# Routed expert tiles: rows read by transposing DMAs from SyncE in place of TensorE transposes

## What is computed

```python
probs = jax.nn.sigmoid(flat @ router_w.T)
scores, idx = jax.lax.top_k(probs, TOPK)
w = scores / (jnp.sum(scores, axis=-1, keepdims=True) + 1e-06)
h = jnp.maximum(jnp.einsum('td,edh->teh', flat, ew1) + eb1[None, :, :], 0.0)
eo = jnp.einsum('teh,eho->teo', h, ew2) + eb2[None, :, :]
routed = jnp.einsum('teo,te->to', eo, comb)
return shared + routed.reshape(b, s, -1)
```

## Time and profile before

| | us |
|---|---|
| median of 3 executions | 700.69 |
| lowest, highest | 696.97, 701.76 |
| profiled execution, its own time | 701.35 |
| its span in the profile | 699.1 |
| routed tiles, first hidden matmul of r0 to the end of r16 | 462.68 to 674.49 |

### The profile page before, as it was taken

The page is one execution under the profiler, slowest core; times in us unless marked ns, Lnnn a source line. Parts: engine busy times, 40 slices in busy tenths (PEclk is TensorE's granted clock), DMA queues, the critical chain, the costliest instruction groups (busy, mean ns, idle before and its releaser), DMA issues. The chain is left out here.

```text
span 699.1 us, 19138 instructions
## 1 busy us (share of the span) xinstructions
PE 601.9 (86%) x6150; PEld 500.8 (72%) x6150; DVE 484.6 (69%) x1304; ACT 394.0 (56%) x994; POOL 287.0 (41%) x327
## 2 busy tenths in 40 slices
PE   2689999999999999999757999989979989899950
PEld 2457777787777778777536888778868878688850
DVE  5858778877877877778695866565654746556537
ACT  4468888888888888887716423253533434324320
POOL 7303344443443334446530077405535534456120
PEclk9799999999999999999975999999999999899995
DMA  8525557775555655633050042213343332441218
GB/s 226 148 79 145 154 135 190 193 187 131 133 133 137 138 141 138 154 87 68 1 181 1 8 153 99 90 42 128 103 154 119 91 120 91 112 145 46 61 49 311
DMA packets 86600, 84.28 MB, mean 121 GB/s; under 512 B 17879, under 2 KB 80341, under 8 KB 86430
## 3 DMA queue, kind: packets, MB, share of 16 engines
q1 hardware_dynamic: 78686, 70.83, 37.5%
q0 software_dynamic: 2976, 8.16, 3.2%
q10 hardware_dynamic: 4896, 4.76, 2.7%
HBM read 55.43 MB, written 28.30 MB: 120 GB/s over the span
## 5 line engine op out<-in xcount | busy, mean ns | idle before, releaser
L928 PE MATMUL ps<-ident,probs 112*125 112x112 f32 x768 | 192.5, 277 | 2.5 <-POOL probs L509 1.4
L714 ACT ACTIVATE probs<-probs,negmax 112x375 f32<-112x375 f32 x256 | 154.9, 608 | 25.9 <-DVE negmax L1230 25.7
L1082 PE MATMUL ps<-w,arena 128*128 128x256 f16 x1152 | 142.1, 280 | 17.7 <-DVE arena L1373 17.3
L764 ACT ACTIVATE arena<-ps,b 128x256 f32<-128x256 f32 x192 | 79.4, 472 | 137.3 <-PE ps L1071 137.1
L928 PEld LDWEIGHTS ps<-ident,probs 112*125 112x125 f32 x768 | 138.8, 188 | 23.7 <-issue 9.0
L1230 DVE CUSTOM_DVE_ANT_0 probs<-ps,neg 112x375 f32<-112x375 f32 x256 | 137.2, 538 | 11.9 <-issue 9.5
L1082 PEld LDWEIGHTS ps<-w,arena 128*128 128x128 f16 x1152 | 111.4, 100 | 43.7 <-DVE arena L1373 29.0
L509 POOL TENSOR_TENSOR probs<-probs,gp_in 112x375 f32<-112x375 f32 x64 | 58.7, 917 | 181.4 <-ACT probs L714 181.4
L1237 DVE TENSOR_TENSOR arena<-ps,gpT 125x336 f32<-125x336 f32 x192 | 97.0, 506 | 46.4 <-PE ps L928 45.8
L1071 PE MATMUL ps<-probs,w 128*128 128x256 f16 x816 | 91.9, 273 | 0.1
L1071 PEld LDWEIGHTS ps<-probs,w 128*128 128x128 f16 x816 | 79.7, 98 | 9.6 <-issue 0.3
(11 more groups left out here) (173 smaller groups left out, 828.9 us busy)
## 6 DMA issues: line engine op xcount, KB each, us to landing
k_scratch<-kT SPq DMA_DIRECT2D x96, 93.8 KB
kst<-k_scratch SPq DMA_DIRECT2D x64, 140.6 KB, 3.6
w1s<-in_L_ffn_ew_dram SPq DMA_DIRECT2D x8, 1024.0 KB, 5.2
w2s<-in_L_ffn_ew_dram SPq DMA_DIRECT2D x8, 1024.0 KB, 5.6
x_sent<-y_sb SPq DMA_DIRECT2D x12, 516.0 KB, 5.5
ctx_in<-in_ctx_dram SPq DMA_DIRECT2D x16, 375.0 KB
probs<-x_sent ACTq DMA_DIRECT2D x18, 258.0 KB
arena<-y_back SPq DMA_DIRECT2D x7, 512.0 KB, 7.2
```

The lines of the kernel that those rows point to most:

```text
L714: act.activation(probs[:, n % PROBS], probs[:, n % PROBS], ACT.Exp, bias=negmax[:, p, n:n + 1], scale=-1.0, accum_out=rowsum[:, p, ORDER[n ...
L764: act.activation(hid32[:, f], ps[:, f // 2 % 4, f % 2 * TILE:(f % 2 + 1) * TILE], ACT.Relu, bias=b1[:, f, e:e + 1]).then_inc(h_relu, 1)
L928: mm = pe.transpose(ps[0:KP, PT[n % 2], c * S:(c + 1) * S], probs[:, n % PROBS, c * KP:(c + 1) * KP], ident[0:S, 0:S])
L1082: mm = pe.matmul(ps[:, 4 + a, 0:D], hid[:, u, f, a * P:(a + 1) * P], w2[:, p, w, f], start=(f == 0 and j == 0), stop=(f == NF - 1 and j == 2))
```

## The change

The rows of a routed tile are no longer read as they are and turned on TensorE. SyncE issues one transposing DMA for each tile (`load_turned`), from `x_sent` straight into `xT`, which has two halves now, for even and odd tiles. It is asked for two tiles ahead, when the hidden matmuls of the tile that used the half are done and the transposing DMA before it has landed. The words come by a DMA of their own (`load_words`, 256 rows of 8 bytes), one tile ahead, after VectorE has used the last ones. `turn_tile`, `take_tile`, `load_tile` and `take_words` are gone. SyncE reads the ends of the experts itself and asks for the upper weights ahead of an expert's tiles and for the lower ones behind them.

```diff
-        xin = probs_all[:, :].bitcast(F16)[:, 0:TILE // P * RW].rearrange("p (a c) -> p a c", c=RW)
-        xT = probs_all[:, :].bitcast(F16)[:, TILE // P * RW:TILE // P * RW + 2 * ND * TILE].rearrange("p (k n) -> p k n", n=TILE)
+        XT = 2 * ND * TILE
+        xT = probs_all[:, :].bitcast(F16)[:, 0:2 * XT]
...
-            load_weights(1)
+            load_up(1)
+            load_down(1)
+
+            def load_turned(r):
+                to = sp.compute_val((r & 1) * XT)
+                sp.dma_start_transpose(xT[:, bass.ds(to, XT)].rearrange("p (k n) -> p k n", n=TILE),
+                                       x_sent[bass.ds(r * TILE, TILE), 0:2 * D]).then_inc(xT_in, 16)
+
+            def load_words(r):
+                sp.dma_start(words_in[:, :, :], x_sent[bass.ds(r * TILE, TILE), 2 * D:RW].rearrange("(a p) c -> p a c", p=P)).then_inc(words_sent, 16)
+
             sp.wait_ge(scattered, 16 * 2 * NT)
-            sp.dma_start(xin[:, :, :], x_sent[0:TILE].rearrange("(a p) c -> p a c", p=P)).then_inc(x_in, 16)
+            load_turned(0)
+            load_words(0)
+            sp.wait_ge(xT_in, 16)
+            load_turned(1)
             sp.wait_ge(tiles_made, 1)
-            for e in range(2, E):
-                load_weights(e)
-            end = sp.value_load(tile_of[0:1, E:E + 1], min_val=E, max_val=RT)
+            end = sp.value_load(tile_of[0:1, 0:1], min_val=0, max_val=RT)
+            for e in range(E):
+                first = end
+                if e + 2 < E:
+                    load_up(e + 2)
+                end = sp.value_load(tile_of[0:1, e + 1:e + 2], min_val=e + 1, max_val=RT)
+                with sp.Fori(first, end) as r:
+                    used, landed, named = sp.compute_val(NF * r + NF * (ST + 1)), sp.compute_val(16 * r + 32), sp.compute_val(2 * r + 1)
+                    sp.wait_ge(in_x[0], 16)
+                    sp.wait_ge(h_mm, used)
+                    sp.wait_ge(in_x[0], 16)
+                    sp.wait_ge(xT_in, landed)
+                    load_turned(r + 2)
+                    sp.wait_ge(in_x[0], 16)
+                    sp.wait_ge(dest_cmp, named)
+                    load_words(r + 1)
+                if e + 2 < E:
+                    load_down(e + 2)
...
             with act.Fori(2, ST) as i:
                 activate(i, E)
-            take_tile(0)
-            act.wait_ge(words_taken, 1)
-            load_tile(1)
...
                 with act.Fori(first, end) as r:
                     activate(r + ST, e)
-                    take_tile(r + 1)
-                    taken = act.compute_val(r + 2)
-                    act.wait_ge(consts, 3)
-                    act.wait_ge(words_taken, taken)
-                    load_tile(r + 2)
...
                 with pe.Fori(first, end) as r:
-                    pe.wait_ge(xT_made, r + 1)
-                    hidden(p, lambda a, k: xT[:, a * ND + k])
-                    turn_tile(r + 1)
+                    at = [pe.compute_val((r & 1) * XT + j * TILE) for j in range(2 * ND)]
+                    turned = pe.compute_val(16 * r + 16)
+                    pe.wait_ge(consts, 3)
+                    pe.wait_ge(xT_in, turned)
+                    hidden(p, lambda a, k: xT[:, bass.ds(at[a * ND + k], TILE)])
                     pe.wait_ge(w2_lo, 1 + W2_CUTS * (e + 1))
                     results(r + ST, p)
...
                     split_hidden(r + ST)
-                    dve.wait_ge(words_taken, r + 1)
+                    dve.wait_ge(words_sent, 16 * r + 16)
                     dve.wait_ge(y_free, r + Y_FREE)
...
                     dve.tensor_scalar(dest[:, 1:2], dest[:, 1:2], 2.0, None, ALU.max).then_inc(dest_cmp, 1)
-                    take_words(r + 1)
```

More of the change, by code:

```diff
@@ L148, in flamingo_block @@
         token_row = sb("token_row", [P, NT], I32)
-        words = sb("words", [P, TILE // P, 2], F32)
+        words_in = sb("words_in", [P, TILE // P, RW - 2 * D], F16)
+        words = words_in[:, :, :].bitcast(F32)
         dest = sb("dest", [P, TILE // P], I32)
@@ L207, in flamingo_block @@
         w1_hi, w1_lo, w2_hi, w2_lo = sem("w1_hi"), sem("w1_lo"), sem("w2_hi"), sem("w2_lo")
[L208 to L209 removed]
+        xT_in, words_sent = sem("xT_in"), sem("words_sent")
         h_mm, h_relu, h_hi, h_split = sem("h_mm"), sem("h_relu"), sem("h_hi"), sem("h_split")
         y_mm, y_made, y_out, y_free = sem("y_mm"), sem("y_made"), sem("y_out"), sem("y_free")
[L212 removed]
+        word_made, dest_cmp = sem("word_made"), sem("dest_cmp")
         back_in = [sem(f"back_in{n}") for n in range(NT // BACK)]
@@ L310, in stack_keys, with load_up @@
                                  ).then_inc(k_in[p][m], 16)
-            def load_weights(e):
+            def load_up(e):
                 if e > 0:
@@ L316, in load_weights, with load_down @@
                 sp.dma_start(w1s[:, :, :], ew1[e].rearrange("(c p) f -> p c f", p=P)).then_inc(in_w1, 16)
+            def load_down(e):
                 if e > 0:
@@ L410, in _ @@
             sp.wait_ge(w2_lo, 1)
-            load_weights(0)
+            load_up(0)
+            load_down(0)
             sp.wait_ge(av_made, H // QUAD * B + AT_FREE)
             sp.dma_start(b2_bc, eb2.partition_broadcast(P)).then_inc(in_b2, 16)
-            load_weights(1)
+            load_up(1)
[4 more added lines that the diff above has]
+                                       x_sent[bass.ds(r * TILE, TILE), 0:2 * D]).then_inc(xT_in, 16)
@@ L423, in _ @@
+            turned, sent = sp.compute_val(end * 16 + 32), sp.compute_val(end * 16 + 16)
+            sp.wait_ge(in_x[0], 16)
+            sp.wait_ge(xT_in, turned)
+            sp.wait_ge(in_x[0], 16)
+            sp.wait_ge(words_sent, sent)
             done = sp.compute_val(end + Y_FREE)
@@ L765, in activate @@
                                    bias=b1[:, f, e:e + 1]).then_inc(h_relu, 1)
-            def take_tile(r):
-                act.wait_ge(xT_mm, r + 1)
-                act.activation(xT[:, :, :], ps[:, 6, 0:2 * TILE].bitcast(F16).rearrange("p (c t) -> p c t", c=2 * ND),
-                               ACT.Copy).then_inc(xT_made, 1)
-            def load_tile(r):
-                act.dma_start(xin[:, :, :], x_sent[bass.ds(r * TILE, TILE)].rearrange("(a p) c -> p a c", p=P)).then_inc(x_in, 16)
             activate(0, E)
@@ L793, in _ @@
                     activate(r + ST, e)
-                    take_tile(r + 1)
-                    taken = act.compute_val(r + 2)
-                    act.wait_ge(consts, 3)
-                    act.wait_ge(words_taken, taken)
-                    load_tile(r + 2)
-            loaded = act.compute_val(end * 16 + 32)
-            act.wait_ge(consts, 3)
-            act.wait_ge(x_in, loaded)
         @block.tensor
@@ L1055, in _ @@
                 route(i)
-            def turn_tile(r):
-                pe.wait_ge(x_in, 16 * r + 16)
-                for a in range(TILE // P):
-                    for c in range(2 * ND):
-                        mm = pe.transpose(ps[:, 6, 0:2 * TILE].bitcast(F16)[:, c * TILE + a * P:c * TILE + (a + 1) * P],
-                                          xin[:, a, c * P:(c + 1) * P], ident16[:, :])
-                mm.then_inc(xT_mm, 1)
             def hidden(p, rows):
@@ L1089, in shared_tile @@
                     rank_pairs()
-                if isinstance(i, int) and i == ST - 1:
-                    turn_tile(0)
                 results(i, 0)
@@ L1414, in _ @@
             dve.wait_ge(in_b2, 16)
-            def take_words(r):
-                dve.wait_ge(x_in, 16 * r + 16)
-                dve.tensor_copy(words[:, :, :], xin[:, :, 2 * D:RW].bitcast(F32)).then_inc(words_taken, 1)
-            take_words(0)
             dve.wait_ge(tiles_made, 1)
```

3 lines of the change are left out of this document (removed).

## The result

The changed kernel takes 691.99 us (median of 10 executions, 689.07 to 696.29); the kernel before takes 697.78 on the same chip (10 executions). The ratio is 0.9914, with a 95% interval of 0.9885 to 0.9942. Measured again with others on another chip it is 0.9892 (0.9858 to 0.9926). So the change wins about 1%, 6 to 8 us, where +0.8 us on the profiled execution of 701.35, that is no change, was forecast.

What follows compares the result with a forecast made beforehand. Collisions of GpSimd's and VectorE's splits and late casts, not the matmuls, were taken as what can be won or lost. 15.0 lost minus 14.2 won gave +0.8 us on 701.35, about 702, range 683 to 722.

Steps and rivals of the forecast that it cites:

- X: Length of an expert's second tile when GpSimd's lower-weight split meets VectorE's split: 16.1 us, between 14.8 and 17.4.
- T: Time by which the transposing DMA, queued on SyncE behind the upper weights, delays y_free: 1.5 us.
- the clock: Clock falling after standstills in a colliding second tile: 14.8 us with it kept, 17.4 with it lost.
- TensorE's transposes go: In undisturbed tiles they fill time VectorE needs anyway: 10.93 to 10.81 us, 0.4 us won in four tiles.
- First tiles 10.8, weights asked for at H + 2.9: Experts' first tiles but r0 fall to 10.81 us by ScalarE's earlier cast; all gains together 14.2 us.
- The lower weights are asked for near the end of an expert ...: nothing: Asking for them near an expert's end, needed 11 us into the next, costs or wins nothing.
- All of r3, r5, r7, r10, r12 collide: In all five second tiles the two splits overlap: 80.5 us against 66.5, 14.0 lost, 15.0 with r14.
- Taking away the late cast takes that luck away: The late cast had let y pass first and spared r5 and r12; without it they collide too.
- SyncE's asks: nothing: SyncE's own issues of some 0.4 us each run beside everything and cost nothing.
- early collisions as in r3: Rival: GpSimd starts as the second tile begins, one pair escapes, second tiles 13.6 us, kernel 690; chance 0.20.
- y passes first: Rival: y's queue gets its share beside the weights, no collisions, second tiles about 11.3 us, kernel 678; chance 0.13.
- The slower rival: The transposing DMA holds the DMA engines; at 5 us of delay, second tiles 20.1 us, kernel 722; chance 0.30.

Runs made afterwards that it cites:

- e2: Changed kernel with plain row loads from SyncE, TensorE's transposes and ScalarE's copy kept: 0.9892 of the kernel before.
- e3: Changed kernel without GpSimd's split of the lower weights for experts 1 to 7: 675.51 us, 0.9642 of the kernel before.
- e1: Changed kernel, SyncE asking for the upper weights only when y of the expert before has landed: 680.42 us, 0.9721 of the kernel before.
- e7: Changed kernel with ScalarE again waiting for dest at each tile's end, so the cast is late: 0.9967 of the kernel before.
- after_again: The changed kernel itself, measured and profiled again on another chip: 0.9892 of the kernel before.
- e10: Changed kernel with the early ask for the lower weights and ScalarE's wait for dest both put back: 1.0101 of the kernel before.
- e14: Changed kernel with plain loads and TensorE's transposes, early ask for lower weights and ScalarE's wait for dest both put back: 1.0114 of the kernel before.
- e6: Changed kernel with the transposing DMA asked for behind dest and the words: 1.0009 of the kernel before.
- e15: Repeat of e6, the changed kernel with the transposing DMA asked for behind dest and the words: 0.9972 of the kernel before.
- e13: Changed kernel with plain loads and TensorE's transposes, early cast, lower weights asked for early again: 1.0065 of the kernel before.
- e4: Kernel before, with SyncE asking for the weights only when y of the expert before has landed: 688.08 us, 0.9828 of the kernel before.

## Why the prediction was wrong

The picture of the first and second tiles was right. The sum failed at the length X of a colliding tile, 16.1 us for a measured 14.64, and X failed through T, the time by which the transposing DMA was to hold up y, and through the clock. Apart from the sum, the gain of the first tiles was of the right size but credited in the main to the wrong part of the change.

- *TensorE's transposes go: 0.4 won.* Undisturbed tiles went from 10.93 to 10.81 to 10.83 (r15, r16), as forecast; but r1 lost 0.4, so that r1, r15 and r16 together lost 0.2. e2 shows that all of this is too small for the ratios.
- *First tiles 10.8, weights asked for at H + 2.9: 14.2 won.* Right in lengths and in sum: 9.6 in the six first tiles, 3.75 in r0 (3.2), 0.75 in r8 (1.0), less the 0.2 of r1, r15 and r16: 13.8. The weights are asked for at H + 2.6. The cause given was wrong in good part, and that the size came out is in so far luck. "The lower weights are asked for near the end of an expert ...: nothing" is the step that failed here: the early ask put back by itself costs 1.3 to 1.7%, the late cast alone 0.3 to 0.8%. In the earlier trace rows the late cast of before was seen, but it wasn't asked why the words ahead of it were late.
- *All of r3, r5, r7, r10, r12 collide.* Right; e3 shows that the split makes them long, and e1 that y behind the weights brings it there. That VectorE's early subtraction also holds the issue of y's first write, so that y comes behind the weights each time, was in the row of r9 (2.28 us) but was not read. "Taking away the late cast takes that luck away" is only partly borne out: with the late cast back (e7), r5 and r12 collide all the same (13.77 and 15.80).
- *T = 1.5.* Failed: 0.2 in one profile, nothing in the other. `y_free` came at H + 9.9 on average (9.2 in `after_again`), not 11.2, since y goes beside the last packets of the weights and beside the transposing DMA. GpSimd began at H' + 0.7 on average (from H' - 0.8 in r10 to H' + 2.0 in r5), not H' + 1.8.
- *X = 16.1.* This is the term on which the sum went wrong: X was 14.64 (14.1 in `after_again`). 5 x (16.1 - 14.64) = 7.3 us, of a forecast of +0.8 for a measured -5.9 (r14 lost 1.3 for a forecast 1.0). The clock fell in two tiles of five (0.90 in r5, 0.89 in r12), where TensorE was busy for 12.67 and 12.54 us instead of 11.0 to 11.2; that makes about 3 us, where the forecast's middle between 14.8 and 17.4 had 5 x 1.3 = 6.5. So about half of the 7.3 is the clock and half the earlier start of the split, as an estimate. The text said that per us of X the time moves by 5, and that was right.
- *SyncE's asks: nothing.* Issues of 0.4 us were forecast; the transposing one takes 1.26, and nothing is seen to wait for it. In e10 and e14, where rows and words stand behind the early ask, they go with a loss of 1%. Whether they cost the changed kernel anything is open; e6 and e15 only show that their place matters by 0.6 to 1.2%.
- *The rivals.* The time came out near the one with early collisions as in r3 (690), with X between its 13.6 and the forecast's 16.1, and by its way: GpSimd began earlier, as T was small. "y passes first" is not what the change did, but what a wait of SyncE does: 680.42 us, where 678 was worked out. The slower rival fell: T never came near 3. A transfer near it in time, the lower weights, does what it was feared for. The rival's case for a fair share rests on the words "the engine round-robins between them" alone; the Trainium skill's same page (DMA: Bandwidth & Descriptors, Queues, rings and completion order) adds that an engine drains a whole packet of one queue, of up to 64 descriptors, before it switches, so it does not promise a small write a prompt turn.

The way from the kernel before to the changed one, in the steps that were run: rows and words from SyncE, with the lower weights still asked for early and the cast late, +1.0 to +1.1%; the cast early -0.3 to -0.8%; the ask for the lower weights late -1.3 to -2.0%; transposing instead of plain loads 0. These add up to the -1% measured, because each step starts where the last one ends; in another order the first step could have another size.

## What to carry to other kernels

Where a small write shares the DMA engines with megabyte loads of another queue and a buffer waits for it, find each load's place relative to that write: moving an ask by some microseconds was worth more here than removing eight TensorE instructions from every tile, and one wait that lets the write go first was worth 2%. Before crediting a gain to the instruction that was seen late, follow its wait back to what was late before it, and cost every moved ask, also those with slack of their own. Put parts of a change back one by one and together, and look at what else the put-back edit moves: a gain of 1% was here made of steps of about -2 and +1.

## What the runs showed of the hardware

- A transposing DMA of 256 rows of 512 fp16 holds SyncE for 1.26 us (a plain one 0.37), lands 3.6 us after its issue, and shows up as many small packets of q1: 509 in one microsecond, with records that overlap (a share of 267.9%). The Trainium skill says that "TRN2 transpose DMAs are as fast as regular DMAs" (Advanced Engine Details and Errata, X-Bar Transpose (TRN2)); the traces agree once the issue is taken off: from the end of its issue a transposing DMA lands in 2.3 us, and a plain load of the same rows in e2, which takes 0.37 to issue and lands after 2.8, in 2.4. Its 1309 ns for each 128x128 block (VectorE: DVE Perf Modes, The three transpose paths) does not add up over eight blocks: that would be 10.5 us, an estimate, and 3.6 were measured.
- GpSimd's packets got no share beside a queue of SyncE full of a megabyte load: none beside 297 packets in e13, none beside 97 in the changed kernel. They passed beside its last packets (61 beside 60), and beside the transposing DMA's small ones (32 beside 509). The Trainium skill's "the engine round-robins between them" (DMA: Bandwidth & Descriptors, SWDGE vs HWDGE vs iDMA), read by itself, fits the second case and not the first; that the size of a packet, as named under the rivals above, is the reason is not shown.
- The issue of a write of y (an indirect DMA on GpSimd) took 2.0 to 3.05 us when it began while VectorE subtracted the upper weights (128x2048, 2.28 us), and it ended 0.83 to 0.86 us behind the subtraction, in all 94 such cases of all profiles. The 518 others took 0.95 to 1.49.
- The kernel before took 698 us beside the result and 700 on the chip of e1 to e4, and 719 to 720 on three other chips. In their profiles r0 begins at 481 to 492 us instead of at 461 to 464: the difference lies ahead of the routed tiles, which take about as long on either (206 and 203 us in two profiles of the changed kernel). The slower ones also ran later, so that it is the chip and not the hour is not shown. Ratios to a kernel measured beside it carry over (0.9914 and 0.9892), times don't.
